# Attention in query halves with batches of four score tiles, folded probability sums, and a regrouped start of the projections

## The chip, the cores and the metric

The kernel runs on one core of a Trainium2 chip. The time is the device time of one execution in microseconds; of the kernel before three runs are known: 1540.91, 1541.34 and 1545.64 us, median 1541.34 us. A core has TensorE (PE, with its weight loads as PEld), VectorE (DVE), ScalarE (ACT), GpSimd (POOL) and SyncE (SP, which here only issues DMAs). Each works through its own instructions in order; they wait for each other by semaphores.

## The reference

The input is `x` (2 batches of 1024 tokens, 512 wide) and a context (2 batches of 2048 tokens, 512 wide). All is float32.

```
xn  = layernorm(x)                                  # (x - mean) / sqrt(var + 1e-5)
lat = layer_norm(xn) * g + b ; ctx = layer_norm(context) * g' + b'
q = lat @ Wq ; k, v = split(ctx @ Wkv)              # 16 heads of 64
k = rope(k, cos, sin)
attn = softmax(clip(q @ k^T / 8, -11, 11))          # over 2048 context tokens
x = x + tanh(g_xattn) * ((attn @ v) @ Wo + bo)
y = layernorm(x)
q8(y) @ q8(rhs) * scales                            # int8 by rows of y and columns of rhs
x = x + tanh(g_ffn) * that
```

So `x` is normalised twice in a row before the q projection, and the exponentials are clipped (`exp` is monotone, so the kernel clips `exp(s)` to `[exp(-11), exp(11)]`) before they are summed and multiplied with `v`.

## The kernel before

It has three stages, each a block of its own with a barrier between.

**Projections** (`projections`). Tokens are taken in chunks of 512 (`CH`), four of `x` (`QCH`) and eight of the context, with two slots. Per chunk: DVE measures mean and variance (`measure`), ACT takes the square root (`sqrt`), DVE normalises in place (`normalise`), PE transposes (`turn`), ACT applies gain and bias (`affine`), DVE splits into a high part and a rest (`tok_split`), and PE multiplies with the weights, split in the same way, three products for one (`split_product`, L220). The chunks of `x` go through `measure`, `sqrt` and `normalise` twice (`passes`), as the reference does. Chunk 0 is treated in two parts (`FRONT`, one tile of 128 tokens, and `BACK`, three). The weights `wq` arrive in two stages of 256 rows each; ACT makes their high part and POOL the rest (L472 to 475), and PE waits for both before its first product (L693, L704). q, k and v go to scratch in DRAM.

**Attention** (`attention`). The 16 heads of each batch are taken in pairs, 16 pairs in all (`ALLPAIRS`), two heads side by side in the 128 partitions. A pair has 16 steps `s` of 128 context tokens. In a step:

- PE, `scores` (L861): for each half of the 1024 queries six matmuls of 64 rows (64 is the head size) by 512 columns, in the two halves of the array's rows, in the fp32r format. A half is one `score_ps` tile of two PSUM banks; there are two.
- ACT, `exps` (L932): one exponential of 128x1024 per half, into one of four slots of `prob`.
- DVE, `pair` (L1022): one clip of 128x2048, in place; then `add_probs` (L1013, L1016): one sum of 128x2048 into `prob_sum`, of the step before, so that it doesn't depend on the clip just issued.
- PE, `values` (L874): four fp32 matmuls of 128 rows, 64 columns of weights and 512 columns, of the step before; each is two passes, so the profile counts eight.

PE's order is scores of step s, values of step s-1. Once a pair, after step 2 of the next, PE sums `prob_sum` over the partitions (`sums`, L887: four fp32 matmuls, eight passes) and ACT copies it out; SP takes the sums through DRAM into 128 partitions, DVE takes reciprocals (L193), SP brings them back broadcast, and DVE multiplies (`normalise`, L204, two of 128x512). SP then stores the pair's output and loads k, q and v of the pair after the next. In the first two pairs DVE also quantises `rhs` (`quantise_rhs`, one small step after each of 24 steps), and in the first POOL makes the rest of `wo` (L1045).

**Output** (`output`): 16 tiles of 128 tokens through `Wo`, normalisation, quantisation and the last product.

## Time and profile before

| | |
|---|---|
| median of three runs | 1541.34 us |
| the profiled execution | 1544.19 us |
| its span, first to last instruction | 1542.4 us |
| projections | to 491.5 us |
| attention | 492.5 to 1423.5 us |
| output | 1423.5 to 1542.4 us |
| PE, DVE, ACT, POOL busy in the span | 97%, 83%, 46%, 8% |
| HBM traffic | 195 MB, 126 GB/s |

The profile comes from one execution, 2.85 us above the median of the runs. Busy shares are an average over three stages that have little in common, so they are read by stage. PE's busy time counts an instruction from when it starts until it is through the array; neighbours overlap, so the spacing of their starts is what one costs.

### The profile page before, as it was taken

What the parts mean: (1) busy time and instruction counts of PE and PEld (TensorE: products, weight loads), DVE (VectorE), ACT (ScalarE), POOL (GpSimd) and SP (SyncE); (2) the same over time, 40 slices, a digit from 0 to 9 for tenths busy, and PEclk for the clock granted to TensorE, in tenths of its full rate; (3) what the DMA queues carried; (4) which work ended last, traced back from release to release, by engine and by line L of the source; (5) the groups of instructions that cost most, each with busy time, mean ns of one, the idle gap of its engine ahead of it and who ended that gap; (6) DMA issues with size and microseconds to landing.
All of it is one profiled execution on the core that took longest, in us unless ns stands there. A gap on an engine that the chain in (4) does not pass through costs nothing. (4 is left out here: it accounts for less than half of the span.)

```text
span 1542.4 us, 22114 instructions
## 1 busy us (share of the span) xinstructions
PE 1490.7 (97%) x7896; PEld 869.5 (56%) x7896; DVE 1287.8 (83%) x1256; ACT 714.5 (46%) x794; POOL 127.8 (8%) x72
## 2 busy tenths in 40 slices
PE   3999999999999899999999999999999999999997
PEld 3788888888886334444444444444444444444774
DVE  6866666676654999899899899899899899998887
ACT  3433222222223555555555555555555555555342
POOL 2220000000000210000000000000000000000765
PEclk9999999999999999999999999999999999999998
DMA  5665655546567540541440440441441442311652
GB/s 185 232 240 190 190 164 181 161 153 200 163 181 256 142 123 29 124 115 38 123 123 28 123 123 27 123 123 38 113 123 46 105 123 55 97 42 35 185 163 82
DMA packets 121998, 195.30 MB, mean 127 GB/s; under 512 B 18368, under 2 KB 67520, under 8 KB 115808
## 3 DMA queue, kind: packets, MB, share of 16 engines
q1 hardware_dynamic: 119360, 190.49, 42.5%
q10 hardware_dynamic: 2592, 4.20, 0.7%
q8 instruction: 28, 0.46, 0.1%
q14 instruction: 18, 0.15, 0.0%
HBM read 114.70 MB, written 79.95 MB: 126 GB/s over the span
## 5 line engine op out<-in xcount | busy, mean ns | idle before, releaser
L932 ACT ACTIVATE prob<-score_ps 128x1024 f32<-128x1024 f32 x512 | 496.3, 1022 | 377.7 <-PE score_ps L861 377.5
L1016 DVE TENSOR_TENSOR prob_sum<-prob_sum,prob 128x2048 f32<-128x2048 f32 x224 | 516.0, 2304 | 0.5
L874 PE MATMUL value_ps<-prob,v_st 128*64 128x512 f32 x2048 | 496.6, 606 | 10.6 <-DVE prob L1022 10.3
L861 PE MATMUL score_ps<-q_st,k_st 64*128 64x512 f32 x3072 | 426.4, 409 | 2.5 <-PEq L102 2.1
L861 PEld LDWEIGHTS score_ps<-q_st,k_st 64*128 64x128 f32 x3072 | 269.2, 185 | 256.4 <-ACT prob L932 187.8
L1022 DVE TENSOR_SCALAR prob<-prob 128x2048 f32<-128x2048 f32 x256 | 314.0, 1226 | 68.1 <-ACT prob L932 64.2
L874 PEld LDWEIGHTS value_ps<-prob,v_st 128*64 128x64 f32 x2048 | 124.2, 136 | 250.1 <-issue 201.7
L645 DVE TENSOR_TENSOR k_cos<-k_raw,rope 128x1024 f32<-128x1024 f32 x32 | 39.2, 1225 | 99.9 <-ACT k_raw L546 99.9
L551 ACT ACTIVATE v_out<-proj_ps 128x1024 f32<-128x1024 f32 x31 | 31.9, 1030 | 136.7 <-PE proj_ps L228 136.7
L546 ACT ACTIVATE k_raw<-proj_ps 128x1024 f32<-128x1024 f32 x31 | 31.9, 1029 | 105.2 <-PE proj_ps L228 104.0
L1331 POOL MEMSET unround<- 128x1 f32 x1 | 0.1, 98 | 872.6 <-POOLq L115 872.6
L228 PE MATMUL proj_ps<-tok_hi,wkv_hi 128*128 128x512 f32 x248 | 67.0, 392 | 0.0
L228 PE MATMUL proj_ps<-wkv_lo,tok_hi 128*128 128x512 f32 x248 | 66.4, 389 | 0.0
L228 PE MATMUL proj_ps<-tok_hi,wkv_lo 128*128 128x512 f32 x248 | 66.3, 389 | 0.0
L228 PE MATMUL proj_ps<-tok_lo,wkv_hi 128*128 128x512 f32 x248 | 66.3, 389 | 0.0
L228 PE MATMUL proj_ps<-wkv_hi,tok_hi 128*128 128x512 f32 x248 | 66.3, 389 | 0.0
L228 PE MATMUL proj_ps<-wkv_hi,tok_lo 128*128 128x512 f32 x248 | 66.3, 389 | 0.0
L228 PEld LDWEIGHTS proj_ps<-tok_hi,wkv_lo 128*128 128x128 f32 x248 | 46.5, 188 | 9.7
L228 PEld LDWEIGHTS proj_ps<-wkv_hi,tok_lo 128*128 128x128 f32 x248 | 46.5, 188 | 9.7
L228 PEld LDWEIGHTS proj_ps<-wkv_lo,tok_hi 128*128 128x128 f32 x248 | 46.5, 188 | 9.7
L228 PEld LDWEIGHTS proj_ps<-wkv_hi,tok_hi 128*128 128x128 f32 x248 | 46.5, 188 | 9.7
L228 PEld LDWEIGHTS proj_ps<-tok_lo,wkv_hi 128*128 128x128 f32 x248 | 46.5, 188 | 9.7
(119 smaller groups left out, 1306.2 us busy)
## 6 DMA issues: line engine op xcount, KB each, us to landing
k_st<-k_scr SPq DMA_DIRECT2D x128, 256.0 KB, 6.2
k_scr<-k_hi SPq DMA_DIRECT2D x64, 256.0 KB, 2.7
v_scr<-v_out SPq DMA_DIRECT2D x32, 512.0 KB, 3.5
k_scr<-k_lo SPq DMA_DIRECT2D x64, 256.0 KB, 4.0
q_st<-q_scr SPq DMA_DIRECT2D x16, 1024.0 KB, 10.5
v_st<-v_scr SPq DMA_DIRECT2D x16, 1024.0 KB, 13.3
q_scr<-q_hi SPq DMA_DIRECT2D x32, 256.0 KB, 3.3
q_scr<-q_lo SPq DMA_DIRECT2D x32, 256.0 KB, 3.4
```

The source lines that it names most:

```text
L228: last = pe.matmul(acc, s, m, start=(n == 0), stop=(n == len(terms) - 1))
L546: act.activation(k_raw[:, j % 2, :, :], banks(what, j, order), ACT.Copy).then_inc(k_copied, 1)
L551: act.activation(v_out[:, j, :], banks(what, j, order), ACT.Copy).then_inc(v_copied, 1)
L645: last = dve.tensor_tensor(made[:, :, :], k_raw[:, s, :, :], rope[:, slot, f:f + 1, :].broadcast_to((P, 2, CH)), ALU.mult)
L861: last = pe.matmul(score_ps[:, half, a, :], k_st[slot][rows, k_part, s * P:(s + 1) * P], q_st[slot][rows, q_part, cols], start=(t == 0), s ...
L874: last = pe.matmul(value_ps[rows, cols], v_st[slot][:, s, rows], prob[:, s % PSLOT, a, cols], start=(s == 0), stop=(s == STEPS - 1))
L932: act.activation(prob[:, s % PSLOT, :, cols], score_ps[:, half, :, :], ACT.Exp, scale=SCALE).then_inc(exped, 1)
L1016: dve.tensor_tensor(total, total, prob[:, s % PSLOT, :, :], ALU.add).then_inc(added, 1)
L1022: dve.tensor_scalar(tile, tile, CLIP_LOW, CLIP_HIGH, ALU.max, ALU.min).then_inc(clipped, 1)
L1331: pool.memset(unround[:, :], -ROUND).then_inc(unround_set, 1)
```

## The change

In the projections: `x` is measured and normalised once; the square root takes `var*(1+eps)+eps^2`, which gives both normalisations at a stroke. Chunk 0 goes tile by tile (`SINGLE`), each with its own DMA. `wq` is staged by halves of its output columns and no longer by halves of its rows, so the first four output tiles need only the first stage; its rest is made by DVE (`wq_rest`), no longer by POOL. PE issues 56 transposes of the identity matrix before chunk 0 is there and 10 after its transposes (`keep_busy`). The tanh of the gates moves from the first instruction of ACT to ahead of the last context chunk.

In attention: a pair is worked in two halves of 512 queries, each over all 16 steps. A unit is one step of one half (six score matmuls, one exponential, two value matmuls); a batch is four units. PE issues the scores of a batch, then the values of the batch before. There are three score tiles of two banks each; `value_ps` and `sum_ps` have one bank each. `prob` has two slots of a batch, the same bytes as before. DVE clips a batch at once (128x4096) and adds its four units as two instructions of 128x2048 into two columns of sums, one for the first batch of a half; after the fourth batch one more addition (128x1024) folds the two into one unit's width. Each addition waits for the instruction ahead of it. `sums` runs once a half on 512 columns for each of two heads, as four matmuls of 256 columns in four groups of 32 columns of the array. The ends of a pair (copies, sums, reciprocals, normalising, stores) come once a half. `quantise_rhs` takes three steps after each batch of pair 0 alone.

```diff
@@ sums to DRAM and back, once a half
-        sp.dma_start(self.sum_scr[n], late.sum_row[0:P:DHEAD, :]).then_inc(late.sum_stored, 16)
+        sp.dma_start(self.sum_scr[n, half], late.sum_row[0:P:SUM_ROWS, :]).then_inc(late.sum_stored, 16)
...
@@ projections
-        for w in range(2):
-            pool.wait_ge(w_hi_made, w + 1)
-            pool.tensor_tensor(wq_lo[:, 2 * w:2 * w + 2, :], w_stage[:, w, :],
-                               wq_hi[:, 2 * w:2 * w + 2, :].bitcast(F32), ALU.subtract).then_inc(w_lo_made, 1)
...
+            act.activation(std[:, tiles], meanvar[:, tiles, 1], ACT.Sqrt, bias=(eps_sq if twice else eps_col)[:, 0:1],
+                           scale=1.0 + EPS if twice else 1.0).then_inc(std_made, 1)
...
-        for p in range(2):
-            measure(0, 0, p, p == 1, FRONT)
-            measure(0, 0, p, p == 1, BACK)
-            normalise(0, p, FRONT)
-            normalise(0, p, BACK)
+        for i, part in enumerate(SINGLE):
+            measure(0, 0, part)
+            if i:
+                normalise(0, 0, SINGLE[i - 1])
+        normalise(0, 0, SINGLE[-1])
+        wq_rest(0)
         tok_split(0, 0)
-        measure(1, 1, 2, False)
+        wq_rest(1)
+        measure(1, 1)
...
+        def keep_busy(times):
+            for i in range(times):
+                pe.transpose(proj_ps[:, 3, 0:P], ident[:, :], ident[:, :])
...
         pe.wait_ge(ident_set, 2)
-        turn(0, 0)
-        pe.wait_ge(w_hi_made, 2)
+        keep_busy(WARM_EARLY)
+        turn_singles()
+        keep_busy(WARM_LATE)
...
@@ attention, PE
+            for u in range(b * BATCH_UNITS, (b + 1) * BATCH_UNITS):
+                half, s = divmod(u, STEPS)
+                cols = slice(half * CH, (half + 1) * CH)
+                if u >= BANKS:
+                    pe.wait_ge(exped, UNITS * n + u - BANKS + 1)
...
-                        last = pe.matmul(score_ps[:, half, a, :], k_st[slot][rows, k_part, s * P:(s + 1) * P],
+                        last = pe.matmul(score_ps[:, u % BANKS, a, :], k_st[slot][rows, k_part, s * P:(s + 1) * P],
...
-                for a in range(2):
-                    last = pe.matmul(sum_ps[a * DHEAD:(a + 1) * DHEAD, cols], ones[:, 0:DHEAD],
-                                     prob_sum[:, slot, a, cols], start=True, stop=True)
+            for a in range(2):
+                for part in range(2):
+                    row = (2 * a + part) * SUM_ROWS
+                    last = pe.matmul(sum_ps[row:row + SUM_ROWS, 0:CH // 2], ones[:, 0:SUM_ROWS],
+                                     prob_sum[:, half, 0, a, part * CH // 2:(part + 1) * CH // 2], start=True, stop=True)
...
+            for b in range(BATCHES):
+                scores(n, slot, b)
+                if b >= 1:
+                    values(n, slot, b - 1)
+                elif not first(n):
+                    values(n - 1, 1 - slot, BATCHES - 1)
+                if b == 1 and not first(n):
+                    sums(n - 1, 1)
+                if b == HALF_BATCHES + 1:
+                    sums(n, 0)
...
@@ attention, ACT
+                if u % BATCH_UNITS == 0 and not (first(n) and b < 2):
+
+                    act.wait_ge(valued, BATCHES * n + b - 1)
+                    act.wait_ge(added, ADDS * (2 * n + (b - 2) // HALF_BATCHES) + 2 * ((b - 2) % HALF_BATCHES) + 1)
+                act.wait_ge(scored, UNITS * n + u + 1)
+                act.activation(prob[:, b % 2, u % BATCH_UNITS, :], score_ps[:, u % BANKS, :, :], ACT.Exp, scale=SCALE
...
@@ attention, DVE
+        def clip(n, b):
+            tile = prob[:, b % 2, :, :]
+            dve.wait_ge(exped, UNITS * n + (b + 1) * BATCH_UNITS)
+            dve.tensor_scalar(tile, tile, CLIP_LOW, CLIP_HIGH, ALU.max, ALU.min).then_inc(clipped, 1)
...
+            for j in range(2):
+                dve.wait_ge(added, before + j)
+                dve.tensor_tensor(total, total, halves[j], ALU.add).then_inc(added, 1)
+            if part == HALF_BATCHES - 1:
+                dve.wait_ge(added, before + 2)
+                dve.tensor_tensor(total[:, 0, :], total[:, 0, :], total[:, 1, :], ALU.add).then_inc(added, 1)
```

PE's order in the second pair, before, around the sums of the first (`score_ps` are the scores, `value_ps` the values; an fp32 matmul stands once here and twice in the profile):

```order
L861 MATMUL score_ps<-q_st,k_st 128x512 x12
L874 MATMUL value_ps<-prob,v_st 64x512 x4
L861 MATMUL score_ps<-q_st,k_st 128x512 x12
L874 MATMUL value_ps<-prob,v_st 64x512 x4
L887 MATMUL sum_ps<-prob_sum,ones 64x512 x4
L861 MATMUL score_ps<-q_st,k_st 128x512 x12
L874 MATMUL value_ps<-prob,v_st 64x512 x4
```

The same place in the changed kernel:

```order
L875 MATMUL score_ps<-q_st,k_st 128x512 x24
L887 MATMUL value_ps<-prob,v_st 64x512 x8
L901 MATMUL sum_ps<-prob_sum,ones 32x256 x4
L875 MATMUL score_ps<-q_st,k_st 128x512 x24
L887 MATMUL value_ps<-prob,v_st 64x512 x8
```

PE passes from scores to values and back once where it did so twice, with the same number of matmuls of either kind; the sums stand twice a pair, at a quarter of the columns in all four groups.

DVE's order in the second pair, before (`prob` is clipped, `prob_sum` is the running sum):

```order
L1022 TENSOR_SCALAR prob<-prob 128x2048
L1016 TENSOR_TENSOR prob_sum<-prob_sum,prob 128x2048
L1022 TENSOR_SCALAR prob<-prob 128x2048
L1016 TENSOR_TENSOR prob_sum<-prob_sum,prob 128x2048
L204 TENSOR_TENSOR o_out<-o_raw,recip 128x512
```

The end of the first half and the start of the second, in the changed kernel's second pair:

```order
L1037 TENSOR_SCALAR prob<-prob 128x4096
L1053 TENSOR_TENSOR prob_sum<-prob_sum,prob 128x2048 x2
L1056 TENSOR_TENSOR prob_sum<-prob_sum 128x1024
L191 RECIPROCAL rec_sq<-sum_sq 128x8
L1037 TENSOR_SCALAR prob<-prob 128x4096
L1049 TENSOR_TENSOR prob_sum<-prob 128x2048
L1037 TENSOR_SCALAR prob<-prob 128x4096
L1053 TENSOR_TENSOR prob_sum<-prob_sum,prob 128x2048 x2
L200 TENSOR_TENSOR o_out<-o_raw,recip 128x512
```

A pair has eight clips for sixteen, fourteen additions of 128x2048 for fifteen, and two of 128x1024 that were not there.

PE's start, before (`turn_ps` are the transposes of chunk 0, `proj_ps` the q projection):

```order
L681 MATMUL turn_ps<-ident,raw 128x128 x4
L687 MATMUL turn_ps<-ident,raw 128x128 x12
L228 MATMUL proj_ps<-tok_hi,wq_hi 128x512 x4
L228 MATMUL proj_ps<-tok_hi,wq_lo 128x512 x4
L228 MATMUL proj_ps<-tok_lo,wq_hi 128x512 x4
```

And in the changed kernel:

```order
L671 MATMUL proj_ps<-ident 128x128 x56
L677 MATMUL turn_ps<-ident,raw 128x128 x16
L671 MATMUL proj_ps<-ident 128x128 x10
L224 MATMUL proj_ps<-tok_hi,wq_hi 128x512 x4
L224 MATMUL proj_ps<-tok_hi,wq_lo 128x512 x4
L224 MATMUL proj_ps<-tok_lo,wq_hi 128x512 x4
```

66 transposes whose result nobody reads are new; the others keep their number and place.

## Rows read from the trace of the kernel before

**Rows 1.** Busy time by stretch: two pairs in attention, then pairs 0 and 1.
```profile
848.72:905.79 57.07, 57.07 (x330) 25.10 (x330) 53.20 (x35) 32.89 (x34) 0.00 (x0) 1.00 0.36 92
...
492.52:560.36 67.84, 59.38 (x334) 26.46 (x336) 61.14 (x39) 38.03 (x42) 16.87 (x5) 0.97 0.42 119
560.36:620.44 60.08, 59.49 (x354) 27.07 (x356) 56.45 (x45) 35.01 (x36) 0.00 (x0) 1.00 0.34 88
```
**Rows 2.** Timeline of PE, two steps: start, length, engine, line, operation.
```profile
801.68 1.94 PE L874 MATMUL value_ps<-prob,v_st 128*64 128x512 f32 x8
803.54 1.65 PE L861 MATMUL score_ps<-q_st,k_st 64*128 64x512 f32 x12
805.13 1.94 PE L874 MATMUL value_ps<-prob,v_st 128*64 128x512 f32 x8
```
**Rows 3.** Timeline of PE in windows inside one step: single pairs of matmuls.
```profile
803.54 0.73 PE L861 MATMUL score_ps<-q_st,k_st 64*128 64x512 f32 x4
...
805.61 0.60 PE L874 MATMUL value_ps<-prob,v_st 128*64 128x512 f32 x2
...
806.04 0.60 PE L874 MATMUL value_ps<-prob,v_st 128*64 128x512 f32 x2
```
**Rows 4.** Timeline of PE, values followed by sums, then scores.
```profile
796.50 1.94 PE L874 MATMUL value_ps<-prob,v_st 128*64 128x512 f32 x8
798.27 1.89 PE L887 MATMUL sum_ps<-prob_sum,ones 128*64 128x512 f32 x8
800.09 0.50 PE L861 MATMUL score_ps<-q_st,k_st 64*128 64x512 f32 x2
```
**Rows 5.** Timeline of DVE in a pair of the loop: normalise, clip, add, clip.
```profile
1240.80 0.68 DVE L204 TENSOR_TENSOR o_out<-o_raw,recip 128x512 f32<-128x512 f32 x1
1241.41 1.22 DVE L1022 TENSOR_SCALAR prob<-prob 128x2048 f32<-128x2048 f32 x1
1242.54 2.28 DVE L1016 TENSOR_TENSOR prob_sum<-prob_sum,prob 128x2048 f32<-128x2048 f32 x1
1244.74 1.22 DVE L1022 TENSOR_SCALAR prob<-prob 128x2048 f32<-128x2048 f32 x1
```
**Rows 6.** Timeline of DVE in the last pair, where the add waits for its clip.
```profile
1377.24 1.22 DVE L1022 TENSOR_SCALAR prob<-prob 128x2048 f32<-128x2048 f32 x1
1378.49 2.29 DVE L1016 TENSOR_TENSOR prob_sum<-prob_sum,prob 128x2048 f32<-128x2048 f32 x1
```
**Rows 7.** Groups of DVE by line and form: busy, mean ns of one.
```profile
L658 DVE TENSOR_TENSOR k_lo<-k_rot,k_hi 128x1024 fp32r<-128x1024 f32 x32 | 39.2, 1226 | 1.1
```
**Rows 8.** Timeline of pair 0: its first exponentials, then a stretch with POOL's work.
```profile
493.52 4.02 ACT L932 ACTIVATE prob<-score_ps 128x1024 f32<-128x1024 f32 x4 [2.05 <-PE score_ps L861]
...
548.25 2.66 POOL L1045 TENSOR_TENSOR wo_lo<-wo_raw,wo_hi 128x1024 fp32r<-128x1024 f32 x1 [4.66 <-ACT wo_hi L957]
548.59 4.46 DVE L1016 TENSOR_TENSOR prob_sum<-prob_sum,prob 128x2048 f32<-128x2048 f32 x1
```
**Rows 9.** Timeline of the start.
```profile
4.81 0.69 DVE L574 BATCH_NORM_STATS2 moments<-raw 128x6 f32<-128x512 f32 x1 [4.81 <-DMA raw<-x_dram]
...
10.57 1.91 ACT L485 ACTIVATE wq_hi<-w_stage 128x2048 fp32r<-128x2048 f32 x1
...
23.27 2.82 PE L687 MATMUL turn_ps<-ident,raw 128*128 128x128 f32 x12 [4.68 <-DVE raw L592]
24.27 2.79 ACT L498 ACTIVATE tok<-turn_ps,gains 128x512 f32<-128x512 f32 x4 [6.84 <-PE turn_ps L687]
...
27.93 2.04 PE L228 MATMUL proj_ps<-tok_hi,wq_hi 128*128 128x512 f32 x4 [1.84 <-DVE tok_hi L601]
```
**Rows 10.** Timeline of PE at the transposes of chunks 1 and 2.
```profile
44.56 1.91 PE L687 MATMUL turn_ps<-ident,raw 128*128 128x128 f32 x16
...
68.28 3.59 PE L687 MATMUL turn_ps<-ident,raw 128*128 128x128 f32 x16 [2.74 <-DVE raw L592]
...
71.61 1.18 PE L228 MATMUL proj_ps<-tok_hi,wq_hi 128*128 128x512 f32 x4
```

More of the change, by code:

```diff
@@ L31 @@
 OT = INNER // P
+SUM_ROWS = P // 4
 EPS = 1e-5
@@ L836, in _ @@
                 n = 2 * i + slot
-                load(n + 2, slot, sp.snap((n + 2) // PAIRS), sp.snap((n + 2) % PAIRS))
-                ends.fetch_reciprocals(sp, n)
-                ends.store_output(sp, n, sp.snap(n // PAIRS), sp.snap(n % PAIRS))
-        sp.wait_ge(late.o_stored, 16 * (ALLPAIRS - 2))
+                here, last, ahead = [(sp.snap((n + d) // PAIRS), sp.snap((n + d) % PAIRS)) for d in (0, -1, 2)]
+                after(n, here, last, (slot,) + ahead)
+        n = ALLPAIRS - 2
+        after(n, (BATCH - 1, PAIRS - 2), (BATCH - 1, PAIRS - 3))
+        for half in range(2):
+            sp.wait_ge(late.o_stored[half], 16 * PAIRS)
         for t in range(2):
@@ new lines, in turn_rhs @@
+        def turn_rhs(part):
+            pe.wait_ge(late.sum_copied, 2)
+            if part == 0:
+                pe.wait_ge(rhs_step, KT + 2 + 3 * KT)
+            else:
+                pe.wait_ge(rhs_copied, 1)
+            for k in range(KT // 2):
+                for t in range(KT):
+                    rows = slice((part * KT // 2 + k) * P, (part * KT // 2 + k + 1) * P)
+                    last = pe.transpose(rhs_ps[:, k, t, :], rhs_int[:, t, rows], ident_bf[:, :])
+            last.then_inc(rhs_turned, 1)
@@ L921, in _ @@
     def _(act):
-        def exps(n, s):
-            for half in range(2):
-                g = STEPS * n + s
-                cols = slice(half * 512, (half + 1) * 512)
-                act.wait_ge(scored, 2 * g + half + 1)
-                if not (first(n) and s < PSLOT):
-                    act.wait_ge(valued, g - PSLOT + 1)
-                    behind = max(s - PSLOT, 1) if s >= PSLOT else s - PSLOT + 1
-                    act.wait_ge(added, (STEPS - 1) * n + behind)
-                act.activation(prob[:, s % PSLOT, :, cols], score_ps[:, half, :, :], ACT.Exp, scale=SCALE).then_inc(exped, 1)
@@ new lines, in pair @@
+        def pair(n, slot):
+            for b in range(BATCHES):
+                clip(n, b)
+                add_probs(n, b)
+                if b == 7 and not (isinstance(n, int) and n == ALLPAIRS - 1):
+                    ends.reciprocals(dve, n, 0)
+                if b == 1 and not first(n):
+                    ends.normalise(dve, n - 1, 0)
+                if b == 3 and not first(n):
+                    ends.reciprocals(dve, n - 1, 1)
+                if b == 5 and not first(n):
+                    ends.normalise(dve, n - 1, 1)
+                if first(n):
+                    for k in range(3):
+                        quantise_rhs(3 * b + k)
```

440 lines of the change are left out of this document (217 added, 223 removed).

## Prediction, made before the changed kernel ran

> **What bounds the kernel now.** I read the slices of the page first, to see that attention fills 931 of the 1542.4 us of the span and that PE is at nine tenths or more nearly everywhere; then busy time by stretch. In a pair of the loop PE is busy for all 57.07 us and DVE for 53.20 [rows 1]: PE sets the pace and DVE follows 4 us behind. The timeline of PE says what PE's time consists of. Values to scores take 1.86 us, scores to values 1.59, a step 3.45 [rows 2]; sixteen are 55.2, and the sums add 1.73: values, sums and the next scores are 3.59 us apart where values alone are 1.86 [rows 4]. Together 57.0, as measured.
>
> The matmuls alone need less. Twelve score matmuls last 1.65 us and the first four 0.73, so a pair of them (two heads side by side) costs 0.23; a pair of value passes costs 0.43 [rows 3]. Six and four of these are 1.38 + 1.72 = 3.10. A step has 0.35 us in which PE changes between tall and wide use of its array.
>
> **Attention, PE.** Matmuls of both kinds keep number and size, and the changes halve. A batch is scores 1.59 + 6 x 0.23 = 2.97 and values 1.86 + 4 x 0.43 = 3.58, so 6.55 us for two steps' work, against 6.90. Eight are 52.4 us a pair. The sums: eight passes of 512 columns, two at a time, fill four slots of 0.43 today. A pass of 256 columns is a slot of 0.215 at best. Four groups at once need two slots, 0.43; two at once 0.86; none 1.72. They also make a third use of the array to change to; a change pair costs 0.35 now, half of it is added here at least, and I take 0.25. So a half costs 0.7, 1.1 or 2.0 us, PE's pair 53.8, 54.6 or 56.4. I take 0.7, since value passes in two groups overlap wholly today.
>
> **Attention, DVE.** From start to start a clip costs 1.13, an add 2.20 and a normalise 0.61 where the next doesn't depend on it [rows 5], and a clip with its add waiting 1.25, 0.03 more than its length [rows 6]. An operation of 1024 columns takes 1.226 [rows 7] and the add of 2048 2.28, so 1.06 go with the columns and 0.17 don't. The clip of 2048, at 1.22, then grows by 1.05 to 2.27 or a little more at 4096; the bounds are 2.27 and twice 1.22, I take 2.29, 2.32 with the wait. An add awaited by the next is 2.28 + 0.04 = 2.32. The fold of 1024 columns is 1.14 to the next. A half: clips 4 x 2.32 = 9.3; adds 2.20 + 2 x (2.32 + 2.20) + 2 x 2.32 = 15.9; fold 1.14; reciprocal 0.17 and normalise 0.61; 27.1 in all. A pair needs 54.2 us of DVE, 1.0 more than today's 53.2 busy, of which the folds are 2.3. PE comes down to 53.8, so DVE takes over as the bound, by 0.4 us. The wait that takes the place of the removed one is thus PE's on clips.
>
> Do the two interlock? ScalarE may begin a batch when DVE has added the batch two before; then DVE does the clip and adds of the batch between, 4.5 us after the first batch of a half and 6.8 or more else. Four exponentials take 4.02 in the first batch of the trace, fed by PE [rows 8]. They fit with 0.5 us to spare at the tightest place, so the clip finds its data. I allow 0.2 us a pair for what slips there, 54.4.
>
> **Attention, the sum.** DVE's chain fixes it. First scores to first clip: 1.0 to the first exponential and 4.0 for four. Pair 0: 54.2, less 1.4 for normalising and a reciprocal that it lacks, plus quantising: twelve steps of 128x512 with one operand at 0.4 (an estimate, below the 0.61 of the normalise of that size with two), four reductions at 0.6, small ones, together 7.5. Plus POOL: beside POOL's 2.66 us an add took 4.46 for 2.28 [rows 8]; four such, 8 to 9; I take 8.1. Today much of both lies in DVE's free 4 us a pair, and pairs 0 and 1 last 67.84 and 60.08 [rows 1]; with DVE as the bound they lie open. Pair 0 then is 68.4. Pair 1 has PE's transposes of `rhs` between batches, 2.5. Tail after the last fold: sums and copy, 1.5. Sum: 5.0 + 68.4 + 15 x 54.4 + 2.5 + 1.5 = 893.4, against 931: **-37.5**.
>
> **The start.** Today chunk 0's last transposes begin at 23.27 and end at 26.1, affine follows, and the products start at 27.93 [rows 9]. With one pass and tiles apart the DVE work before the transposes is four measures, four small steps and four normalises, some 1.6 us a tile from 4.8 on (a measure alone is 0.69 [rows 9]): the last tile is ready near 11.3. PE is then still warming: 56 transposes are 12.2 us at the slow spacing of 0.22 (16 in 3.59) and 6.2 at the fast 0.11 (16 in 1.91) [rows 10]. Started near 2.1 they end at 14.3 if the clock never rises, near 10.6 if it rises after 4.7 us. Then come 16 transposes, affine's 2.79 and the split. With the clock up: ScalarE is on `wq_hi` until 12.5 [rows 9], affine to 15.3, products from 16.1, 11.8 earlier. With it down: transposes to 17.8, products from 20.9, 7.0 earlier. DVE's `wq_rest` (2.29, as an add of that size) lies in the 3 us in which it awaits affine.
>
> Which? The row to read is 68.28: PE had idled for 2.74 us, its clock went to 1.2 GHz for that stretch (16 transposes in 3.59), and when nothing but those transposes had run the next matmuls went at 2.4 GHz (four in 1.18) [rows 10]. Transposes raised the clock here. The Trainium skill, "TensorE: Matmul & The Clock Gate", Part 4 (PE-mode transpose), says the opposite, that full clock doesn't engage for transposes, as they don't count as busy in the same way. By it the start brings 7.0, by the row 11.8; it is a rival below.
>
> Between the ten last transposes and the products lie some 3 us of idle PE, as long as the gap that let the clock fall at 68.28. So I credit 1.0 of the slow first 5.3 us (four products in 2.04 for 1.18). Then the stall itself: PE waited 2.74 for the second pass over chunk 2, and its transposes took 3.59 for 1.91. That pass is gone, so 4.4 more. Start and projections: 11.8 + 1.0 + 4.4 = **-17**. The rest of the projections stays PE-bound with PE always busy. The tanh now ahead of the last chunk lies in one of the gaps in which ScalarE, 46% busy over the span, waits for PE; if that gap were too short it would cost some 1.5 us. The output stage I leave at 119 us.
>
> **Sum.** 1542.4 - 37.5 - 17 = 1487.9 in the span; the profiled execution stands 1.8 over its span, 1489.7, and 2.85 over the median: **1486 us**, 3.6% faster.
>
> **Rivals.**
> *The sums don't overlap as thought.* The trace has two column groups at work, never four, and no passes of 256. With none at once PE's pair is 56.4: 15 x 2.0 more, 1516; two at once 1489. For it: a group of 32 columns is new. Against: the two groups of today overlap completely.
> *Alternation is not what costs.* If the 0.35 us belong to a unit's waits on its score tile rather than to the change, 32 units pay as now: PE 16 x 3.45 + 1.4 = 56.6, time 1519. For it: each group of six matmuls still has a wait. Against: the second six of a step, which wait as well, show no gap.
> *Transposes don't warm the clock.* 4.8 later, plus the 1.0: 1492.
> *Slower than before: two slots of `prob` starve DVE.* The place is the first exponential of a batch, which waits for values and adds two batches back; with ScalarE and the clip in line behind it, each 0.1 us by which four exponentials, a copy of values or sums and the semaphores outlast DVE's work on the batch between stands open. The price is 128 batches: it turns the gain of 55 into a loss from 0.43 us a batch; at 0.8 us the time is 1588. For it: a clip now waits for four exponentials where it waited for two, spare 0.5 us. Against: only one batch in four is that tight, the others have 2.8.
> *Nothing gained in attention*, DVE's waits being dearer than 0.03: it needs 2.7 us over 22 waits a pair, 0.12 each; 1524.
>
> **Chances.** The forecast with two or four groups at once and either clock: 0.60, itself 1476 to 1496. Sums alone 0.10, alternation 0.09, small interlock and dear waits between 1496 and 1530 0.13, starvation past the old time 0.05, and 0.03 for a time below 1476 (quantising and POOL better hidden). The range runs from 1474 to 1517. A measurement here tells 0.3% (4.6 us) from no change. Faster 0.93, same 0.02, slower 0.05.
>
> **What would show it.** Pairs 54.4 us apart in the copies of values; DVE busy at 98% and more in attention and PE waiting a few tenths for clips: the forecast. PE full and DVE with gaps: sums or alternation, told apart by the sums' row (0.6 long or 2) and by the scores' spacing in a batch (24 in 3.2 us). DVE idle before clips, released by ScalarE: starvation. First products near 16 us, four in 1.2 or 2.0. No PE gap ahead of chunk 2's transposes. It is wrong if attention is shorter than 885 us or longer than 900, or if products start after 21 us.

## The result, and the profile after

The changed kernel takes 1495.68 us (median of 5, 1494.51 to 1498.57) against 1541.34; the ratio is 0.970, 95% interval [0.968, 0.971]. It is 45.7 us faster, and 9.7 above the forecast of 1486, inside its range of 1474 to 1517.

The profiled execution took 1494.74 us with a span of 1492.8. Stage by stage, from the first row of each stage in the timeline of PE (the forecast's terms for the start are rounded to 17 in its total):

| stretch, us | before | after | change | forecast |
|---|---|---|---|---|
| start to first products | 27.93 | 16.40 | -11.5 | -11.8 |
| products to first scores | 464.59 | 457.60 | -7.0 | -5.4 |
| attention | 931.04 | 897.33 | -33.7 | -37.5 |
| output | 118.80 | 121.44 | +2.6 | 0 |
| span | 1542.4 | 1492.8 | -49.6 | -54.5 |

Busy time by stretch, the changed kernel: two pairs of the loop, then 400 us of attention. The columns are the window, its length, then busy us and instructions of PE, PEld, DVE, ACT and POOL, the granted clock, DMA.
```profile
849.23:904.19 54.96, 53.82 (x338) 25.82 (x340) 53.75 (x29) 32.16 (x36) 0.00 (x0) 1.00 0.39 96
904.19:958.92 54.73, 53.82 (x338) 25.68 (x340) 53.29 (x29) 32.17 (x37) 0.00 (x0) 1.00 0.38 96
...
900.00:1300.00 400.00, 393.34 (x2454) 187.76 (x2452) 390.93 (x206) 235.90 (x265) 0.00 (x0) 1.00 0.37 94
```
These answer to [rows 1]. A pair fell from 57.07 to 54.84 (the mean of the two), and the roles changed: PE now has gaps of one us a pair. Its own timeline in the loop, with values, sums and scores:
```profile
907.53 3.65 PE L887 MATMUL value_ps<-prob,v_st 128*64 128x512 f32 x16 [0.41 <-DVE prob L1037]
911.12 0.64 PE L901 MATMUL sum_ps<-prob_sum,ones 128*32 128x256 f32 x8
911.69 3.04 PE L875 MATMUL score_ps<-q_st,k_st 64*128 64x512 f32 x24
...
918.25 3.06 PE L875 MATMUL score_ps<-q_st,k_st 64*128 64x512 f32 x24
921.24 3.65 PE L887 MATMUL value_ps<-prob,v_st 128*64 128x512 f32 x16
924.83 1.43 PE L875 MATMUL score_ps<-q_st,k_st 64*128 64x512 f32 x10
```
Scores to values 2.99 us, values to scores 3.59: 6.58 for a batch of two steps (forecast 6.55; two steps of [rows 2] are 6.90). Sums to scores 0.57 for a half (forecast 0.7). The wait in brackets is the new one: PE waits for a clip.

DVE, timeline of the loop:
```profile
909.74 2.29 DVE L1037 TENSOR_SCALAR prob<-prob 128x4096 f32<-128x4096 f32 x1
912.17 4.62 DVE L1053 TENSOR_TENSOR prob_sum<-prob_sum,prob 128x2048 f32<-128x2048 f32 x2
```
and of the last pair, which is written out behind the loop:
```profile
1347.24 2.29 DVE L1037 TENSOR_SCALAR prob<-prob 128x4096 f32<-128x4096 f32 x1
1349.57 4.62 DVE L1053 TENSOR_TENSOR prob_sum<-prob_sum,prob 128x2048 f32<-128x2048 f32 x2
```
The clip of 4096 columns lasts 2.29 as forecast. From its start to the add that awaits it there are 2.33 us in the last pair, as forecast, and 2.40 to 2.43 in the loop. That is the only price of DVE in the loop that was missed: the second of two adds awaits the first in both places, and two take 4.62 us in both.

The start, timeline of PE, which answers to [rows 9, 10]:
```profile
2.12 7.64 PE L671 MATMUL proj_ps<-ident 128*128 128x128 f32 x56 [2.12 <-POOL ident_bf L459]
9.60 2.46 PE L677 MATMUL turn_ps<-ident,raw 128*128 128x128 f32 x16
11.90 1.25 PE L671 MATMUL proj_ps<-ident 128*128 128x128 f32 x10
16.40 1.17 PE L224 MATMUL proj_ps<-tok_hi,wq_hi 128*128 128x512 f32 x4 [3.25 <-DVE tok_hi L586]
...
51.37 1.91 PE L665 MATMUL turn_ps<-ident,raw 128*128 128x128 f32 x16
```
And the end of attention, the same view:
```profile
1369.81 0.78 PE L901 MATMUL sum_ps<-prob_sum,ones 128*32 128x256 f32 x8 [2.26 <-DVE prob_sum L1056]
1371.33 3.75 PE L1216 MATMUL wo_ps<-wo_hi,o_hi 128*128 128x512 f32 x8 [0.74 <-PEq L116]
```
Eight matmuls of `wo_ps` in 3.75 us are at 1.2 GHz; at 2.4 GHz they take 2.06 (below). The granted clock from 1369.81 to 1375.10 was 0.54. DVE's last addition leaves PE idle for 2.26 us there and the change of stage for 0.74 more, and the output stage begins slow.

### The profile page after: what moved, and what is told of

Same layout as the page of the kernel before. It is cut to its first block and busy times, and to the rows that moved or that the text cites. A ratio compares the mean times of both kernels' runs of the same rounds, so it can differ in the third digit from the quotient of the medians.

```text
span 1492.8 us, 22563 instructions
## 1 busy us (share of the span) xinstructions
PE 1447.1 (97%) x8090; PEld 884.9 (59%) x8090; DVE 1273.3 (85%) x1108; ACT 700.0 (47%) x823; POOL 118.9 (8%) x71
## 5 line engine op out<-in xcount | busy, mean ns | idle before, releaser
L953 ACT ACTIVATE prob<-score_ps 128x1024 f32<-128x1024 f32 x512 | 482.9, 1031 | 193.6 <-PE score_ps L875 186.0
L887 PE MATMUL value_ps<-prob,v_st 128*64 128x512 f32 x2048 | 469.4, 600 | 18.4 <-DVE prob L1037 18.4
L1053 DVE TENSOR_TENSOR prob_sum<-prob_sum,prob 128x2048 f32<-128x2048 f32 x192 | 446.2, 2324 | 14.5 <-DVE prob L1037 1.8
L875 PE MATMUL score_ps<-q_st,k_st 64*128 64x512 f32 x3072 | 394.9, 402 | 8.7 <-ACT prob L953 6.6
L887 PEld LDWEIGHTS value_ps<-prob,v_st 128*64 128x64 f32 x2048 | 136.8, 137 | 287.6 <-issue 276.1
L1037 DVE TENSOR_SCALAR prob<-prob 128x4096 f32<-128x4096 f32 x128 | 291.3, 2275 | 12.8 <-ACT prob L953 12.7
L1049 DVE TENSOR_TENSOR prob_sum<-prob 128x2048 f32<-128x2048 f32 x32 | 75.8, 2368 | 2.9 <-DVE prob L1037 0.2
L966 ACT ACTIVATE sum_row<-sum_ps 128x256 f32<-128x256 f32 x32 | 12.3, 385 | 95.3 <-PE sum_ps L901 95.3
```

Source lines behind the costliest of these rows:

```text
L875: last = pe.matmul(score_ps[:, u % BANKS, a, :], k_st[slot][rows, k_part, s * P:(s + 1) * P], q_st[slot][rows, q_part, cols], start=(t == ...
L887: last = pe.matmul(value_ps[rows, :], v_st[slot][:, s, rows], prob[:, b % 2, i, a * CH:(a + 1) * CH], start=(s == 0), stop=(s == STEPS - 1))
L953: act.activation(prob[:, b % 2, u % BATCH_UNITS, :], score_ps[:, u % BANKS, :, :], ACT.Exp, scale=SCALE).then_inc(exped, 1)
L1037: dve.tensor_scalar(tile, tile, CLIP_LOW, CLIP_HIGH, ALU.max, ALU.min).then_inc(clipped, 1)
L1049: dve.tensor_tensor(total, halves[0], halves[1], ALU.add).then_inc(added, 1)
L1053: dve.tensor_tensor(total, total, halves[j], ALU.add).then_inc(added, 1)
```

## The experiments

The theory: PE's time was the matmuls' own and that of the array changes, which halved; DVE's chain now sets the pair (54.84), with 0.09 us too much in each of eight waits; PE's clock gives 2 us back or takes them at gaps. Eleven kernels, each timed in turns with the kernel before. Pair is the mean distance of pairs 2 to 14 in the copies of the second half's values. Pair, attention and output come from the profiled execution, which can stand a few us off the median.

| kernel | median us | ratio to before, 95% | pair | attention | output |
|---|---|---|---|---|---|
| the changed kernel | 1495.68 | 0.970 [0.968, 0.971] | 54.82 | 897.3 | 121.4 |
| two-unit turns | 1587.49 | 1.031 [1.029, 1.033] | 60.59 | 990.2 | 120.2 |
| no fold | 1490.41 | 0.968 [0.966, 0.969] | 54.68 | 894.7 | 118.8 |
| two groups | 1495.80 | 0.971 [0.969, 0.973] | 54.85 | 901.5 | 121.0 |
| no warming | 1495.43 | 0.971 [0.969, 0.973] | 54.82 | 897.3 | 120.3 |
| constant waits | 1487.59 | 0.964 [0.963, 0.966] | 54.08 | 889.2 | 121.2 |
| clip in two | 1487.35 | 0.964 [0.963, 0.966] | 54.03 | 889.1 | 121.3 |
| rest on VectorE | 1491.83 | 0.967 [0.966, 0.969] | 54.78 | 896.7 | 118.8 |
| joined | 1487.99 | 0.965 [0.964, 0.966] | 54.29 | 891.0 | 120.3 |
| PE kept busy | 1491.95 | 0.968 [0.967, 0.970] | 54.82 | 898.4 | 118.8 |
| joined, constants | 1480.40 | 0.960 [0.959, 0.962] | 54.08 | 885.9 | 118.7 |
| joined, split | 1479.91 | 0.960 [0.959, 0.961] | 54.03 | 884.6 | 118.8 |

### Does alternation cost what was said? (two-unit turns)

```
-                scores(n, slot, b)
-                    values(n, slot, b - 1)
+                for part in range(2):
+                    scores(n, slot, b, part, 2)
+                        values(n, slot, b - 1, part, 2)
```


> The changed kernel, but PE takes two units of scores, then two units of values, in turn, so it alternates as often as the kernel before; nothing else differs. Theory (each change between tall and wide use costs, 0.35 us for a there and back): a batch is 6.90 us of PE for 6.55, a pair 52.4 + 8 x 0.35 + 1.2 = 56.4, PE is the bound again with DVE showing gaps before clips, and the time rises by 15 x 1.6 = 24 us to about 1519. Rival (the 0.35 us belong to the waits of a unit on its score tile, of which there are as many as before): PE's pair stays 53.8 us of work, the pair stays 54.8 and the time 1496.

(The two functions got the bounds of a part of the batch; those lines are left out.) Timeline of PE in its loop:
```profile
908.05 1.65 PE L875 MATMUL score_ps<-q_st,k_st 64*128 64x512 f32 x12
909.64 1.94 PE L888 MATMUL value_ps<-prob,v_st 128*64 128x512 f32 x8
911.50 1.65 PE L875 MATMUL score_ps<-q_st,k_st 64*128 64x512 f32 x12
```
A step is 1.59 + 1.86 = 3.45 again, to the hundredth that of [rows 2]. Over 400 us:
```profile
900.00:1300.00 400.00, 375.31 (x2220) 164.47 (x2216) 356.14 (x186) 217.68 (x238) 0.00 (x0) 1.00 0.34 87
```
PE is busy for 375.31/400 of a pair of 60.59, 56.8 us, where the changed kernel has 393.34/400 x 54.84 = 53.9. So 2.9 us a pair are eight changes there and back (8 x 0.35 = 2.8): the alternation is shown as the place of PE's gain. What in a change takes the time, no run shows. The time itself, 1587, is 68 above the 1519 of the theory, and not for PE's work: PE is idle for 24.7 us here. The waits of the same stretch (us in total, times, longest):
```profile
DVE prob L1040 <- ACT prob L956: 35.2, 23, 2.7
PE value_ps L888 <- DVE prob L1040: 24.6, 39, 1.4
```
The timeline of PE, ACT and DVE shows the ring behind them:
```profile
921.73 1.94 PE L888 MATMUL value_ps<-prob,v_st 128*64 128x512 f32 x8 [1.38 <-DVE prob L1040]
923.60 1.66 PE L875 MATMUL score_ps<-q_st,k_st 64*128 64x512 f32 x12
924.61 1.94 ACT L956 ACTIVATE prob<-score_ps 128x1024 f32<-128x1024 f32 x2 [2.97 <-PE score_ps L875]
...
926.58 2.29 DVE L1040 TENSOR_SCALAR prob<-prob 128x4096 f32<-128x4096 f32 x1 [2.66 <-ACT prob L956]
```
The first half of a batch's values waits for its clip, the second half of the next batch's scores stands behind those values in PE's order, ScalarE waits for these scores, and the next clip waits for ScalarE. DVE starves, as in a rival of the forecast, but at another place: the rival had the first exponential of a batch waiting for a free slot of `prob`, and here it is the third, waiting for PE. So the run says nothing of how much slack two slots leave. It says that scores which stand behind values that wait for a clip cost 3.7 us of idle PE a pair.

### What are the fold and the four groups worth? (no fold; two groups)

```
-            if part == HALF_BATCHES - 1:
-                dve.tensor_tensor(total[:, 0, :], total[:, 0, :], total[:, 1, :], ALU.add)
+                    for j in range(2):
+                        last = pe.matmul(..., prob_sum[:, half, j, a, ...], start=(j == 0), stop=(j == 1))
```


> The changed kernel without the fold: DVE leaves the two columns of sums, and PE adds both in PSUM (eight matmuls of 256 columns a half for four). Theory (DVE is the bound by about 1 us a pair, and a half of the sums costs PE 0.57 us): DVE's pair falls by 2.3 to 52.5 us, PE's rises by 2 x 0.43 to 54.7, so PE takes over and the pair stays within 0.3 us of 54.8: time 1490 to 1498, DVE with gaps. Rival (DVE alone bounds and PE has room): the pair falls by 2 us or more, time 1465. Rival (four groups don't overlap when two matmuls add up in one group): PE's sums take 2.3 us or more a half, time above 1510.

```
-                for part in range(2):
-                    last = pe.matmul(sum_ps[row:row + SUM_ROWS, 0:CH // 2], ones[:, 0:SUM_ROWS], ...)
+                last = pe.matmul(sum_ps[a * DHEAD:(a + 1) * DHEAD, :], ones[:, 0:DHEAD], prob_sum[:, half, 0, a, :])
```


> The changed kernel with the sums as before in shape: two matmuls of 512 columns a half in two groups of 64 columns of the array, no third use of the array. Theory (four groups work fully side by side): PE's sums take 0.86 us a half for 0.57, PE's pair 54.4 for 53.8, still below DVE's 54.8, so the time stays within 4 us of 1496. Rival (PE and DVE bound the pair together, so that every addition to PE shows): 15 x 0.6 = 9 us more, 1505.

Timelines of PE, sums and the scores behind them, without the fold:
```profile
911.16 1.09 PE L902 MATMUL sum_ps<-prob_sum,ones 128*32 128x256 f32 x16
912.18 3.06 PE L875 MATMUL score_ps<-q_st,k_st 64*128 64x512 f32 x24
```
its busy time:
```profile
900.00:1300.00 400.00, 400.00 (x2580) 192.63 (x2578) 374.90 (x192) 236.75 (x266) 0.00 (x0) 1.00 0.37 93
```
With two groups, the timeline around the sums:
```profile
910.59 3.65 PE L887 MATMUL value_ps<-prob,v_st 128*64 128x512 f32 x16
914.07 1.03 PE L899 MATMUL sum_ps<-prob_sum,ones 128*64 128x512 f32 x4
915.04 3.04 PE L875 MATMUL score_ps<-q_st,k_st 64*128 64x512 f32 x24
```
Sums to scores are 1.02 us for twice the passes in four groups, 0.97 in two groups, 0.57 in the changed kernel. With slots of 0.215 for 256 columns and 0.43 for 512 that is 4 x 0.215, 2 x 0.43 and 2 x 0.215, and 0.16, 0.11 and 0.14 over. So four fp32 groups of 32 columns do run at once: 0.57 us is less than two at a time would need (0.86). Changing to the third form costs some 0.14 rather than the 0.25 that I took.

Two groups need no third form, so the sums also start sooner behind the values. From values over sums to scores they take 4.45 us (910.59 to 915.04) and the changed kernel 4.16 (907.53 to 911.69): 0.6 us of PE a pair, as the theory had it, and the time is the same (1495.80). PE had that much idle; over 400 us it is busy for 397.48 in place of 393.34. That this profile's attention is 4.2 us longer is not the sums' work in the loop, where the pair is 54.85. Half of it is pair 1 (58.13 us between first clips for 56.07): behind 2.46 us of idle PE, as long as in the changed kernel, 16 value passes took 5.35 us for 3.65, at a granted clock of 0.68. Most of the rest lies at the end, from the last pair on.

Without the fold DVE has 16 us less in 400 and PE is full, as the theory said; the loop is no slower (54.68) and the median 5 us lower. In the profiles attention is 2.6 shorter, by pair 0, where DVE's chain is open (65.48 between the first clips of pairs 0 and 1 for 68.40), and the output stage 2.6: DVE hands over its last sum sooner, PE's last gap is 1.00 us and not 2.26, and the clock stays up. That the shorter gap kept it up is likely and not shown, since one profile below has a fast output stage behind 2.26 us. The fold costs time, and the four groups bring nothing that can be measured beside batches and halves.

### Does the warming work? (no warming; PE kept busy)

```
-    WARM_EARLY = 56
-    WARM_LATE = 10
+    WARM_EARLY = 0
+    WARM_LATE = 0
```


> The changed kernel without the 66 idle transposes at the start. Theory (transposes raise the clock, and it stays up until the products): PE's first products start near 16.3 us as now, since the tiles of chunk 0 set that, but at 1.2 GHz, four in about 2.0 us for 1.2, for some 3.4 us or more; attention starts 2 to 4 us later than 474.0 and the time is about 1499. Rival (transposes don't raise the clock and the fast first products have another cause): no difference, 1496.

Its timeline of PE at the start:
```profile
10.54 1.97 PE L677 MATMUL turn_ps<-ident,raw 128*128 128x128 f32 x8 [0.33 <-DVE raw L577]
16.35 2.04 PE L224 MATMUL proj_ps<-tok_hi,wq_hi 128*128 128x512 f32 x4 [3.84 <-DVE tok_hi L586]
...
21.60 1.23 PE L224 MATMUL proj_ps<-tok_hi,wq_hi 128*128 128x512 f32 x4
```
Products at the spacing of 1.2 GHz until 21.6, and attention starts at 476.10 for 474.00; the granted clock reads 1.00 there, so the level is read from the durations. First products come at 16.35 without any warming and at 16.40 with it, so the 11.5 us that the start gained owe nothing to the clock. What the single pass, the tiles apart and the new staging of `wq` each brought was not separated. The theory's 1499 did not come: the median is that of the changed kernel, the rival's number, though not for the rival's reason. The kernel without the fold has all 66 warming transposes and shows why:
```profile
11.53 1.26 PE L671 MATMUL proj_ps<-ident 128*128 128x128 f32 x10
16.36 2.05 PE L224 MATMUL proj_ps<-tok_hi,wq_hi 128*128 128x512 f32 x4 [3.58 <-DVE tok_hi L586]
```
Warm, that is at 2.4 GHz, at 11.53 (ten in 1.26) and cold, at 1.2 GHz, at 16.36 (four in 2.05), behind 3.58 us of idle PE. Of eight profiles with these warmers (the changed kernel and seven others) one only, the changed kernel's own, shows attention at 474.0; the others have 474.8 to 476.4. In five of those seven the first twelve products take 5.26 us, as without warming and as before the change (3.27 in the changed kernel's profile), in the other two 4.1 to 4.2. So the gap takes back most or all of what the transposes earned. Filling it:

```
-    WARM_LATE = 10
+    WARM_LATE = 24
+        for i in range(18):
+            pe.transpose(sum_ps[:, 0:P], ident[:, :], ident[:, :])
         sums(ALLPAIRS - 1, 1)
```


> Two gaps of TensorE are filled with transposes of the identity whose results nobody reads: WARM_LATE 24 for 10 ahead of the first products (2.6 us of them at the fast spacing for 1.1), and 18 ahead of the last sums (2.0 us in a gap of 2.26). Everything else is the changed kernel's. Theory (the clock falls in these gaps in some executions and not in others, and each time it costs about 2 us): the first products go four in 1.2 us and attention starts at 474.0, where it started 476.1 to 476.3 in the other runs; the output stage lasts 118.8 where the changed kernel's profile shows 121.45, its first eight matmuls 2.08 and not 3.75. Time 1495.7 less 2.6 less up to 2.1: 1491 to 1493, with less spread. Rival (the clock stands at what the stretch before has earned, and transposes of this size don't hold it): starts and output as before, 1495.5, and 1497 if the longer filling delays the products.

```profile
11.97 2.78 PE L671 MATMUL proj_ps<-ident 128*128 128x128 f32 x24
16.22 1.17 PE L224 MATMUL proj_ps<-tok_hi,wq_hi 128*128 128x512 f32 x4 [1.47 <-DVE tok_hi L586]
...
1368.49 2.18 PE L944 MATMUL sum_ps<-ident 128*128 128x128 f32 x18
```
Products at 2.4 GHz, attention from 473.83, output 118.8: 1491.95, the theory's 1491 to 1493. The three profiles with both fillings (this one and the last two below) all start attention at 473.8 to 474.0 and have an output stage of 118.7 to 118.8. In these runs transposes raised the clock (the first of the 56 start 0.21 us apart, the last 0.11) and held it. The Trainium skill, "TensorE: Matmul & The Clock Gate", Part 4 (PE-mode transpose), says that full clock doesn't engage for them; by that these 24 and 18 would have changed nothing, and the measurement decides against it.

One gap stays, the 2.11 us between the last projection and the first scores. Busy time of the first 2 us of attention, here and in the changed kernel's profile:
```profile
473.83:475.83 2.00, 2.00 (x10) 1.73 (x12) 0.00 (x0) 0.31 (x1) 0.00 (x0) 0.50 0.53 217
474.00:476.00 2.00, 2.00 (x18) 1.82 (x18) 0.00 (x0) 1.00 (x2) 0.00 (x0) 1.00 0.52 217
```
At a granted clock of 0.50 the first clip comes 5.87 us after the first scores, at 1.00 after 4.81. Of the twelve kernels with the changed attention four show the fast case in their profile and eight the slow one. This gap was never filled.

### What does DVE's loop cost? (constant waits; clip in two)

```
-        all_pairs(dve, pair)
+        for n in range(ALLPAIRS):
+            pair(n, n % 2)
```


> VectorE's loop over the pairs is written out, so that its waits compare with constants and not with a register; its work and its order stay, and so does everything on the other engines. In the loop of the changed kernel an add that awaits its clip starts 2.40 to 2.43 us after the clip (909.74 to 912.17, 917.31 to 919.72), in the last pair, which is written out, 2.32 (1347.24 to 1349.57). Theory (VectorE sets the pace, and 0.09 us of a pair's eight such waits is the register's price): a pair of 54.84 loses 0.7 and comes to about 54.1, times 14 pairs is 10 us, 1486 us. Rival 1 (TensorE with its 53.8 us and its short waits sets the pace as much as VectorE): the pair stays above 54.6 and the time at 1493 to 1496. Rival 2 (code that isn't looped over costs instruction loading on VectorE): gaps between its instructions of over 0.1 us that the loop doesn't have, 1496 or more.

```
-            dve.tensor_scalar(tile, tile, CLIP_LOW, ...).then_inc(clipped, 1)
+            for j in (0, 2):
+                dve.tensor_scalar(tile[:, j:j + 2, :], tile[:, j:j + 2, :], CLIP_LOW, ...).then_inc(clipped, 1)
```


> Each clip of 128x4096 is issued as two of 128x2048. The first add of a batch waits for the first of them, which ended while the second ran, and the second add for the second, which is then long done; the loop stays a loop. Theory (what a dependent neighbour costs VectorE is more than an instruction's fixed part): two clips at 1.13 us from start to start are 2.26 for 2.41 now, 0.15 less in each of 8 batches, 1.2 us a pair, which brings VectorE's need to 53.6, under TensorE's 53.8; the pair ends at 53.9 to 54.1 and the time at 1483 to 1486. Rival (the 0.17 us of an instruction that don't go with its columns come on top of what the wait costs): 8 x 0.17 more against 8 x 0.09 less, a pair of 55.3 and 1503 us.

With constants, DVE's timeline, and PE's where a half begins:
```profile
908.46 2.29 DVE L1037 TENSOR_SCALAR prob<-prob 128x4096 f32<-128x4096 f32 x1
910.79 4.62 DVE L1053 TENSOR_TENSOR prob_sum<-prob_sum,prob 128x2048 f32<-128x2048 f32 x2
```
```profile
930.19 3.06 PE L875 MATMUL score_ps<-q_st,k_st 64*128 64x512 f32 x24
933.39 1.94 PE L887 MATMUL value_ps<-prob,v_st 128*64 128x512 f32 x8
```
From clip to add there are 2.33 us in place of 2.43, and the pair is 54.06 between the first clips. DVE still sets it: a half's operations follow one another without idle time and take 27.03 us (903.98 to 931.01). PE needs some 53.7 (an estimate from its rows: eight batches at 6.57 and two sums at 0.57). Its waits for clips, 6.7 us in 400 (14 times) in the changed kernel, are too short for the list now, but once a half its values still start behind a late clip, 3.20 us after the scores for 2.98 elsewhere. The median fell by 8.1 us for the 10 of the theory. From first clip to last add it was 9.5, the twelve pairs of the loop at 0.8; the first clip came 1.1 later after the first scores (5.91 us for 4.80, the slow clock there), and this profile's start was cold. So DVE did bound the pair. No gaps came with the longer code.

The price is not the register's alone, since the second add of the loop also awaits its neighbour and starts 0.03 us behind it. The instructions of DVE's sequencer at these two adds, in the changed kernel's loop and with constants (from 909 and 908 to 915 and 916; kind, number, ns min/median/max, first and last start):
```profile
L1052 DVEq FUSED_REGOPS  x1: 64/64/64, 912.1 to 912.1; - x1
...
L1052 DVEq EVENT_SEMAPHORE  x2: 21/21/21, 908.6 to 915.4; - x2
```
The code awaits two semaphores ahead of the first add, `clipped` and `added`. By the records of the two traces the add itself carries one wait, and an instruction of the sequencer ahead of it the other. In the loop the wait for the clip is on the register operation: it starts when the clip has ended at 912.02, lasts 0.06, and the add follows at 912.17, 0.15 behind the clip. With constants the separate instruction awaits `added`, which is raised by then, and runs at 908.6 during the clip; the add awaits the clip itself and starts 0.03 behind it. So what costs is that the wait which ends last stands on an instruction of its own.

The clip in two, DVE's timeline:
```profile
908.71 2.36 DVE L1038 TENSOR_SCALAR prob<-prob 128x2048 f32<-128x2048 f32 x2
910.98 4.61 DVE L1056 TENSOR_TENSOR prob_sum<-prob_sum,prob 128x2048 f32<-128x2048 f32 x2
```
2.27 from clips to adds inside the loop (2.44 where a half begins, 904.06 to 906.50). A second instruction is cheaper than a neighbour's wait. Pairs take 53.94 and 54.05 in turn. That is again DVE's own chain, 27.02 us a half without idle time (904.06 to 931.08), and not PE's floor: of the theory's 1.2 us 0.8 came, since the first add of a half still waits, and 0.07 us longer than before the edit.

### Pair 0 and POOL (rest on VectorE; joined)

```
-            pool.tensor_tensor(late.wo_lo[:, rows, :], wo_raw[:, :, :], ...)
+                if first(n) and b in WO_BATCHES:       # (1, 3, 5, 7), was (1, 3, 4, 5)
+                    dve.tensor_tensor(late.wo_lo[:, 2 * w:2 * w + 2, :], wo_raw[:, :, :], ...)
```


> The four subtractions that make wo_lo (128x2048 each), in the first pair on GpSimd today, go to VectorE behind batches 1, 3, 5 and 7. In the changed kernel three of VectorE's adds beside them lasted 6.66 to 6.68 us in place of 4.62 for the two, a fourth 4.34 for 2.3: about 8.1 us of VectorE's chain in pair 0. Theory (VectorE is the bound there, and the contention is exposed): 8.1 goes, 4 x 1.2 comes (1226 ns for 1024 columns; if they are 2048 columns in length, 4 x 2.3 comes, and then +1), so 3 us less in pair 0 and 1492.5 us, with pair 0 at 66.9 from 70.06; or 1496.5 with 71 if the longer duration holds. Rival (the first pair is bound by something else, quantising's waits for ScalarE): pair 0 longer by what is added, 74.8 and 1500.

In the changed kernel, POOL's subtraction and DVE's adds beside it:
```profile
487.29 3.28 POOL L1083 TENSOR_TENSOR wo_lo<-wo_raw,wo_hi 128x1024 fp32r<-128x1024 f32 x1 [4.76 <-ACT wo_hi L991]
...
486.03 6.68 DVE L1053 TENSOR_TENSOR prob_sum<-prob_sum,prob 128x2048 f32<-128x2048 f32 x2
```
and on DVE instead, where the two adds ahead of it take 4.62:
```profile
493.90 1.22 DVE L1065 TENSOR_TENSOR wo_lo<-wo_raw,wo_hi 128x1024 fp32r<-128x1024 f32 x1
```
Pair 0, from first clip to first clip, 64.99 for 68.40: 3.4 less, where 3 was forecast. The Trainium skill, "SBUF — State Buffer", section "SBUF: two separate sides", says that an operation of VectorE with two inputs and one of GpSimd that reads SBUF lock each other out; the trace agrees, with 2.06 us more for two adds. But pair 1 became longer by 2.6 (58.67 for 56.07), which I had not foreseen (timeline of PE, then busy time of that stretch with the granted clock behind POOL's columns):
```profile
549.48 6.24 PE L887 MATMUL value_ps<-prob,v_st 128*64 128x512 f32 x16 [3.60 <-DVE prob L1037]
```
```profile
549.48:555.70 6.22, 6.22 (x20) 1.71 (x24) 6.19 (x3) 0.00 (x0) 0.00 (x0) 0.58 0.91 213
```
The piece behind batch 7 lengthened PE's wait from 2.46 to 3.60 us, and 16 passes ran in 6.24 us for 3.65, at a granted clock of 0.58. The length of the wait is likely the cause but not the whole of it: the two profiles with 3.60 us there are both slow behind it, and of the eight with 2.45 to 2.49 us one is, that of two groups. So the first two pairs gave 0.8 between them, and the median fell by 3.9. The rest in this profile is a fast output stage (118.8 us), though the gap of 2.26 us is there too; nothing in the edit touches that end, so I put it down to chance.

> The last three together: clips in two, VectorE's loop written out, wo_lo on VectorE. If TensorE's 53.8 us of a pair is the floor that comes up when VectorE gets faster, the pair is 53.9 to 54.0 whatever of the two edits on VectorE's waits brought it there, and the time is 1483 less what the third brings, 1479 to 1484. If the floor is lower than thought (TensorE's 53.82 busy contains waits that the profile books as work), the pair comes under 53.7 and the time under 1478.

1487.99, no better than its parts. Start and pair 1 are cold (first scores at 476.36, pair 1 58.67), and the pair is 54.27: two adds take 4.60 us to the next operation against 4.53, six times a pair, and the first adds of a half start 0.09 sooner. The place is the second add: it starts 0.10 us behind the first where the other loops have 0.03. In the trace an instruction of the sequencer of its own awaits the first add there (0.02 us long, at 913.81, behind the add's end at 913.77) and the second add carries the wait for its clip, long done. It is the same effect as in the loop of the changed kernel, with the waits the other way round; the last pair of the kernel with split clips alone, which is written out, has the same 0.10.

> VectorE's loop written out (constant waits), wo_lo on VectorE but behind batches 1, 3, 4 and 6 rather than 7, and the two gaps filled as in the run above. Theory (the parts are independent): from 1487.6 of the written-out loop alone 2.1 at the start, 2.5 at the output stage and 3.4 in the first pair come off, 1479 to 1481; pair 1 has no values at half speed and lasts 56.1 between the first clips as in the changed kernel (58.67 with the piece behind batch 7, where TensorE idled for 3.60 us and its next 16 values took 6.24 for 3.65). Rival (VectorE's added work in the first pair just opens another gap of TensorE, in which the clock falls): pair 0 or 1 keeps 2.6 us, 1483.

> As the run above, but with each clip in two and VectorE's loop kept in place of the written-out loop. Theory: a pair of 54.0 as the clip in two had alone (53.94 and 54.05 in turn), 1478 to 1481. Rival (what made the joined version slower, 54.27 a pair for 54.06, is wo_lo's place and not the two edits of waits together): 54.27 again and 1483.

With the piece behind batch 6, both gaps filled and one of the two edits of waits: 1480.40 and 1479.91, both as forecast and not to be told apart; pair 1 is 56.07 and 56.19. That is 15 to 16 us, 1%, under the changed kernel and 4.0% under the one before.

## Why the prediction was right, and where its numbers were off

The mechanism is the forecast's: PE's pair fell by the array changes that were taken out, DVE took over as the bound, and PE waits a few tenths for clips. Attention, 897.3 us, lies inside its 885 to 900. DVE is busy for 97.7% of the 400 us and not for 98, as its waits are longer.

*Start and projections, -17, measured -18.5.* The last tile was ready at 11.35 (forecast 11.3), products came at 16.40 (16.1), the stall before chunk 2's transposes is gone, and these take 1.91 for 3.59. The 1.0 credited for the clock was less than this profile shows (none of the first products at 1.2 GHz, about 2.5 us) and more than five of the other seven with these warmers do, whose first twelve products took 5.26 us as before the change. The 20.9 that I had for the first products with the clock down holds only because slow warming transposes would have stood in chunk 0's way; without any warming the products start at 16.35.

*PE in attention, 53.8 a pair.* Measured 53.82 busy in a window of one pair, 53.7 by the spacing of its rows. Batch 6.58 for 6.55; sums 0.57 for 0.7, their overlap and the third form's change both measured.

*DVE in attention, 54.2 and 0.2 that slip.* Pair 0 came to 68.4 between first clips, exactly as summed, and the written-out pairs of the constant waits to 54.06. The term that was too small is the wait of an add for its clip in the loop: I took 0.03 us from the last pair of [rows 6], which is written out, and in the loop it is some 0.09 more, since there a register operation of the sequencer carries the wait. Eight of them are the 0.7 us a pair which I had at 0.2. Attention became 3.9 longer than the 893.4 of the sum: 15 pairs took 822.6 us for 818.5. The twelve pairs of the loop are 5.5 over, pair 1 and the two last ones 1.5 under. The rival of dear waits was right in kind with a quarter of its size: 0.7 us a pair where it needed 2.7, in eight of its 22 waits.

*Output, 0, measured +2.6.* This term was put at nothing without a reason. DVE as the bound ends attention with PE idle for 2.26 and 0.74 us, where before they were 0.39 and 1.38; the output stage then starts at 1.2 GHz in most profiles (in seven of the nine without the filling). I had looked for the clock at the start and not at the other end.

*The span, +4.9 over forecast, and the median.* Against the forecast's terms -1.5 at the start, +3.8 in attention and +2.6 in the output stage make the 4.9. The other 4.8 lie in the last step: I subtracted 2.85, as the profiled execution of before stood that much over its median, and the profiled one of after stood 0.9 below, 3.8 in all; and my sum gives 1486.9, which I wrote down as 1486. A single execution's distance to the median is not to be carried over. With the first products at the slow clock, as in most of the later profiles, the span would have been some 2 us further off.

*The rivals.* Four groups of sums overlap, the change of the array is what cost, and transposes raise the clock. With four-unit turns DVE does not starve; with two-unit turns it does, by PE's order and not by the slots of `prob` that the rival named. That its 1588 for 0.8 us a batch is near that run's 1587 is chance.

## What to carry to other kernels

Count the changes between forms of TensorE's array: 0.35 us there and back here, and eight fewer were worth 2.9 of TensorE's 57 us a pair. When a change takes the bound from TensorE to another engine, read what that engine pays per wait inside a loop, from rows of the loop itself and not from a written-out tail; and where an instruction awaits two semaphores, see to it that the one raised last is awaited by the instruction itself (a trace shows which wait stands where). And list TensorE's gaps at the ends of stages: behind some of them it ran at 1.2 GHz for a while, which cost 1 to 3 us each, and a few idle transposes in the gap held the clock in all three profiles that had them.

## What the runs showed of the hardware

- A VectorE instruction that carries the wait for its neighbour itself starts 0.03 us behind its end, in a loop or not. Where an instruction of the sequencer ahead of it carries that wait, it starts 0.10 us behind (constants) or 0.12 to 0.15 (a register operation, in the loop).
- Four fp32 groups of 32 columns run wholly at once: 8 passes of 256 columns in 0.57 us, 16 in 1.02.
- Behind gaps of about one length the clock stood at either level: 2.26 us (and 0.74) were followed by eight matmuls in 3.75 us in one profile and in 2.06 in another; 2.46 us by 16 value passes in 5.35 and in 3.65; 3.25 us by four products in 1.17, and 3.04 by four in 2.04.
- GpSimd's subtraction of 128x1024 lengthens two adds of VectorE from 4.62 to 6.68 us and itself takes 3.28, where VectorE does it in 1.22.
